# Attention after a convolution on one core: minus the maximum by one step of eight 32x64 tiles, dumps folded by DMAs, value halves added by TensorE

## What is computed

```
h = group_norm1(x, n2_g, n2_b)
q, k, v = conv1x1(h, q_w, q_b), conv1x1(h, k_w, k_b), conv1x1(h, v_w, v_b)   # each (B, 64, N)
attn = softmax(einsum('bnc,bcm->bnm', q, k) * 64 ** -0.5, axis=-1)           # (B, N, N)
out = x + einsum('bnm,bmc->bnc', attn, v)
```

## Time and profile before

| | |
|---|---|
| median of 3 runs | 3047.66 us (3044.29 to 3048.20) |
| the profiled execution | 3046.7 us |
| its span, first to last instruction | 3045.0 us |
| busy: TensorE / VectorE / ScalarE / GpSimd | 90% / 65% / 73% / 76% |
| granted TensorE clock, mean | 0.96 of full speed |

### The profile page before, as it was taken

The page is one execution under the profiler, slowest core; times in us unless marked ns, Lnnn a source line. Parts: engine busy times, 40 slices in busy tenths (PEclk is TensorE's granted clock), DMA queues, the critical chain, the costliest instruction groups (busy, mean ns, idle before and its releaser), DMA issues.

```text
span 3045.0 us, 87180 instructions
## 1 busy us (share of the span) xinstructions
PE 2736.0 (90%) x36568; PEld 1138.5 (37%) x36568; DVE 1967.6 (65%) x2081; ACT 2218.4 (73%) x2288; POOL 2311.9 (76%) x2056
## 2 busy tenths in 40 slices
PE   7898999998989898999988989999999999999998
PEld 4343333333333333333333333333333333333333
DVE  4766666666666666666657666666666666666665
ACT  4577777777777777777767777777777777777777
POOL 1467777777778787877865878787888888887886
PEclk9999999999999999999999999999999999999999
DMA  6148666666666666666601656666666666666561
GB/s 195 35 102 182 130 131 128 129 126 129 132 127 131 128 131 127 131 133 126 122 7 41 130 125 135 132 129 130 130 135 134 134 135 134 134 135 128 124 128 21
DMA packets 124020, 371.20 MB, mean 122 GB/s; under 512 B 17640, under 2 KB 43752, under 8 KB 123120
## 3 DMA queue, kind: packets, MB, share of 16 engines
q0 software_dynamic: 88128, 320.90, 51.8%
q1 hardware_dynamic: 35504, 44.75, 5.5%
HBM read 16.41 MB, written 9.44 MB: 8 GB/s over the span
## 4 chain that ended last, share of the span: by engine, by line
PE 36%; POOL 21%; issue 13%; DVE 11%; DMA 11%; ACT 6%; POOLq 0%; ACTq 0%; SPq 0%; DVEq 0%
POOL arena L486 17%; PE ps L1060 16%; PE ps L1049 12%; DMA accD<-arena 11%; DVE mxp L827 6%; PE ps L1069 5%; ACT arena L576 3%; POOL accD L501 2%; DVE arena L853 2%; POOL mseed L519 2%; ACT ps L617 2%; PE ps L1182 2%; DVE accD L850 1%; ACT pvx L591 1%; DVE pvc L874 1%
## 5 line engine op out<-in xcount | busy, mean ns | idle before, releaser
L827 DVE TENSOR_REDUCE mxp<-ps 128x1 f32<-128x1024 f32 x1296 | 1581.0, 1224 | 775.2 <-PE ps L1069 774.1
L486 POOL TENSOR_TENSOR arena<-arena 128x512 f32<-128x512 f32 x1224 | 1703.2, 1391 | 417.7 <-ACT arena L576 351.9
L576 ACT ACTIVATE arena<-ps,bnd 128x1024 f32<-128x1024 f32 x1296 | 1382.0, 1110 | 502.3 <-PE ps L1049 483.8
L1060 PE MATMUL ps<-arena,vals 64*64 64x512 f32 x10368 | 1294.6, 613 | 0.2 <-DVE pvc L874 0.2
L1049 PE MATMUL ps<-arena 64*64 64x512 f16 x15552 | 1087.0, 382 | 145.1 <-ACT ps L617 140.1
L617 ACT ACTIVATE ps<-mseed 128x1024 f32<-128x1024 f32 x612 | 628.8, 1027 | 176.6 <-POOL mseed L519 125.5
L1049 PEld LDWEIGHTS ps<-arena 64*64 64x64 f16 x15552 | 463.1, 108 | 589.8 <-issue 322.1
L1069 PE MATMUL ps<-arena,QM 64*64 64x512 f16 x5184 | 528.5, 395 | 121.8 <-DVE mxp L827 116.9
L501 POOL DMA_DIRECT2D accD<-arena x544 | 494.4, 910 | 94.2 <-DMA accD<-arena 56.4
L1060 PEld LDWEIGHTS ps<-arena,vals 64*64 64x64 f32 x10368 | 385.0, 137 | 419.9 <-issue 333.7
L1069 PEld LDWEIGHTS ps<-arena,QM 64*64 64x64 f16 x5184 | 153.5, 105 | 664.1 <-DVE mxp L827 574.3
(11 more groups left out here) (124 smaller groups left out, 807.1 us busy)
## 6 DMA issues: line engine op xcount, KB each, us to landing
accD<-arena POOLq DMA_DIRECT2D x612, 512.0 KB, 5.1
arena<-arena SPq DMA_DIRECT2D x144, 64.0 KB, 3.5
arena<-in_x_rows SPq DMA_DIRECT2D x8, 816.0 KB, 9.7
xs<-in_x SPq DMA_DIRECT2D x4, 1152.0 KB, 15.5
f_scratch<-arena SPq DMA_DIRECT2D x32, 144.0 KB
f<-f_scratch SPq DMA_DIRECT2D x16, 288.0 KB, 9.7
QM<-arena SPq DMA_DIRECT2D x72, 64.0 KB, 3.5
xst<-arena SPq DMA_DIRECT2D x72, 64.0 KB, 4.4
```

The lines of the kernel that those rows point to most:

```text
L486: nc.gpsimd.tensor_tensor(accA[:, n % 2, :], accA[:, n % 2, :], e, ALU.add).then_inc(adda_free, 1)
L576: nc.scalar.activation(E[:, :, slot_of(n % 2, p), :], ps[:, S_BANK + 2 * buf:S_BANK + 2 * buf + 2, :], ACT.Exp, scale=bnd[:, 6:7]).then_in ...
L827: nc.vector.reduce_max(flat(mxp[:])[:, v:v + 1], flat(ps[:, bank:bank + 2, :]), AX.X).then_inc(mx_free, 1)
L1060: a = nc.tensor.matmul(ps[C * t:C * t + C, ACC_BANK + r, :], V[rows, p, t, :], E[rows, t, slot_of(par, p), :], start=(p == 0), stop=(p == ...
```

## The change

`place_minus_maxima` takes the place of the fourth term and of all fills. One step of eight matmuls on tiles of 32 x 64 writes minus the maximum to the four score banks of both pairs of a turn, and three terms of each pair are added to it. It waits for the exponential of pair p+1 before it writes. `seed`, `fill_source`, `is_seeded` and `mseed` go.

Dumps are issued after each odd pair of their own block, into one of two `accD` by turns. In the next block, after pairs 5, 8 and 11 (`FOLD_AFTER`), GpSimd's queue issues three accumulating DMAs: half of `accD` onto the other, then its two parts onto `accA` (`fold_dumps`). `sum_dumps` goes, and `total` stays for the last block of a batch.

The row sums are taken at pair 18 instead of 12. Behind them TensorE adds the two halves of the values with weights `twice` (two identity matrices, one above the other) into the other half of the same bank (`value_sums`), and ScalarE copies both at once. `turn_pv` and `sum_pv` go. `add_pv` stands behind the first reduction of a block, not ahead of it. GpSimd multiplies after pair 31. VectorE's reciprocals come one a pair. In the stretch between the batches the same steps shift by some chunks (not shown), and at the very end VectorE multiplies straight from PSUM.

```diff
@@ -52,19 +52,19 @@
 K_ROWS = KW + 1
 
 AHEAD = 4
-ROW_SUMS = 12
+ROW_SUMS = 18
 
 LASTS = NBLK - 1
-DUMP_AFTER = (8, 9, 11, 12, 14, 15, 17, 18, 20, 21, 23, 25, 27, 29, 31, 33, 35, 35)
-NDUMP = len(DUMP_AFTER)
-DUMPS_SUMMED = 6
+NDUMP = NPAIR // 2
+FOLD_AFTER = (5, 8, 11)
+NFOLD = len(FOLD_AFTER)
 RECS = 8
-SEEDED = (0, 1)
 QK_TOP = 2.0 ** 14
 
 ROUNDING = 1.0 + 2.0 ** -10
 ONE = 2.0 ** 14
-M_ROW = 1.0 / (ONE * 64)
+ROWS = 32
+M_ROW = 1.0 / (ONE * ROWS)
 
 
 def program(nc, x, x_rows, conv_w, per_row, per_channel, matrices, matrices_t, out):
...
             def dump(b, j, g):
 
-                n, k = blk(b, j), g % 2
+                n, k, d = blk(b, j), g % 2, dumped_block(b, j)
                 at = slot_of(n % 2, 2 * g)
                 pool.wait_ge(e_ready, NPAIR * n + 2 * g + 3)
                 if g >= 2:
                     pool.wait_ge(dumped[k], dumps_before(b, j, g))
-                    pool.dma_start(accD[:, k, :], E[:, 1, at:at + 2, :].rearrange("p s c -> p (s c)"), accum_op=ALU.add
+                    pool.dma_start(accD[:, d % 2, k, :], E[:, 1, at:at + 2, :].rearrange("p s c -> p (s c)"), accum_op=ALU.add
                                    ).then_inc(dumped[k], 16)
                 else:
-                    if n:
-                        pool.wait_ge(accb_out, n)
-                    pool.dma_start(accD[:, k, :], E[:, 1, at:at + 2, :].rearrange("p s c -> p (s c)")).then_inc(dumped[k], 16)
-
-            def total(n):
-
+                    if d:
+                        pool.wait_ge(dumped[k], dumps_before(b, j, g))
+                    if d >= 2:
+                        pool.wait_ge(folded, folds_before(d - 1, 0))
+                    pool.dma_start(accD[:, d % 2, k, :], E[:, 1, at:at + 2, :].rearrange("p s c -> p (s c)")
+                                   ).then_inc(dumped[k], 16)
+
+            def fold_dumps(b, j, i):
+
+                n, d = blk(b, j), dumped_block(b, j)
+                if i == 0:
+                    for k in (0, 1):
+                        pool.wait_ge(dumped[k], dumps_before(b, j + 1, 0))
+                    pool.dma_start(accD[:, d % 2, 0, :], accD[:, d % 2, 1, :], accum_op=ALU.add).then_inc(folded, 16)
+                else:
+                    pool.wait_ge(folded, folds_before(d, i))
+                    pool.wait_ge(adda_free, NSLOT + NPAIR * (n + 1))
+                    pool.dma_start(accA[:, n % 2, :], accD[:, d % 2, 0, (i - 1) * CH:i * CH], accum_op=ALU.add
+                                   ).then_inc(folded, 16)
+
...
             def attend(b, j):
                 n = blk(b, j)
-                fill_source(n)
                 first_a(n)
-                for p in range(2, NPAIR):
-                    add_a(n, p)
-                    if j < LASTS:
-                        for g in range(NDUMP):
-                            if DUMP_AFTER[g] == p:
-                                dump(b, j, g)
-                    if j and p == DUMPS_SUMMED + 2:
-                        total(n - 1)
-                    if j and p == 33:
-                        pool.wait_ge(rec_ready, RECS * n)
-                        pool.wait_ge(pv_summed, 2 * n)
-                        nc.gpsimd.tensor_tensor(pvt[:], pvt[:], rec[:], ALU.mult).then_inc(norm_done, 1)
+                for p in range(1, NPAIR):
+                    if p > 1:
+                        add_a(n, p)
+                    if j < LASTS and p % 2:
+                        dump(b, j, p // 2)
+                    if j and p in FOLD_AFTER:
+                        fold_dumps(b, j - 1, FOLD_AFTER.index(p))
+                    if j and p == 31:
+                        normalize(n - 1)
...
                 nc.scalar.activation(flat(pvc[:]), ps[:, ACC_BANK, :], ACT.Copy).then_inc(acc_copied, 1)
-
-            def turn_pv(n):
-
-                act.wait_ge(acc_free, n + 1)
-                for h in (0, 1):
-                    nc.scalar.activation(pvx[C * h:C * h + C, :], pvc[C - C * h:2 * C - C * h, h, :], ACT.Copy).then_inc(pv_turned, 1)
 
             def copy_row_sums(n, bank):
                 act.wait_ge(rs_ready, n + 1)
                 if n:
                     act.wait_ge(rec_ready, RECS * n)
-                nc.scalar.activation(rsum[:], ps[:, bank, 0:HCH], ACT.Copy).then_inc(rs_copied, 1)
+                    act.wait_ge(norm_done, n)
...
                         copy_row_sums(n - 1, S_BANK)
-                    if p + 2 < NPAIR and is_seeded(b, p + 2):
-                        seed(b, j, p + 2)
                     if p == 1 and j:
                         move_pv(n - 1)
-                    if p == 4 and j:
-                        turn_pv(n - 1)
                     if p == NPAIR - 3 and j + 1 < NBLK:
                         widen_maxima(n + 1)
                     if p == NPAIR - 1 and j + 1 < NBLK:
...
                         add_b(b, n, p + 1)
-                    if j and p == 10:
-                        sum_pv(n - 1)
-                    if j and p == DUMPS_SUMMED:
...
@@ -1032,22 +1005,28 @@
                 pe.wait_ge(st_in, n + 2)
                 nc.tensor.matmul(ps[:, bank, 2:3], of[:], dev[:, 1:2], start=True, stop=True).then_inc(st_ps, 1)
 
-            def scores(par, p, peers, seeds=None):
+            def place_minus_maxima(par, peers):
 
                 if peers is not None:
                     pe.wait_ge(e_ready, peers + 1)
+                for r in (0, 2, 1, 3):
+                    rows = slice(ROWS * r, ROWS * r + ROWS)
+                    for h in (0, 1):
+                        cols = slice(C * h, C * h + C)
+                        nc.tensor.matmul(ps[cols, S_BANK + 2 * (r % 2) + r // 2, :], one16[rows, cols], QS[rows, par, 2, :],
+                                         start=True, stop=False, skip_group_check=True, tile_position=(ROWS * r, C * h))
+
+            def scores(par, p):
+
                 keys = slice(p * P, (p + 1) * P)
-                terms = ((KH[:, keys], 0), (KL[:, keys], 0), (KH[:, keys], 1), (one16[:], 2))
-                if seeds is not None:
-                    pe.wait_ge(seeded, seeds)
-                    terms = terms[:3]
+                terms = ((KH[:, keys], 0), (KL[:, keys], 0), (KH[:, keys], 1))
                 for k, (of, part) in enumerate(terms):
                     for t in (0, 1):
                         rows = slice(C * t, C * t + C)
                         for h in (0, 1):
                             cols = slice(C * h, C * h + C)
                             a = nc.tensor.matmul(ps[cols, S_BANK + 2 * (p % 2) + t, :], of[rows, cols], QS[rows, par, part, :],
-                                                 start=(k == 0 and seeds is None), stop=(k == len(terms) - 1),
+                                                 start=False, stop=(k == len(terms) - 1),
                                                  skip_group_check=True)
                 a.then_inc(s_ready, 1)
 
...
+
+            def value_sums(n, bank):
+                pe.wait_ge(acc_free, n + 1)
+                for h in (0, 1):
+                    a = nc.tensor.matmul(ps[C * h:C * h + C, bank, HCH:CH], twice[:], pvc[:, h, :], start=True, stop=True)
                 a.then_inc(rs_ready, 1)
 
-            def row_sums(n, bank):
-                pe.wait_ge(sum_ready, n + 1)
+            def row_sums(b, j, bank):
+                n = blk(b, j)
+                if j < LASTS:
+                    pe.wait_ge(folded, folds_before(dumped_block(b, j) + 1, 0))
+                    sums = accA[:, n % 2, :]
+                else:
+                    pe.wait_ge(sum_ready, b + 1)
+                    sums = accS[:]
                 for h in (0, 1):
-                    a = nc.tensor.matmul(ps[C * h:C * h + C, bank, 0:HCH], ones[:, 0:C],
-                                         accS[:, h * HCH:(h + 1) * HCH], start=True, stop=True)
-                a.then_inc(rs_ready, 1)
+                    nc.tensor.matmul(ps[C * h:C * h + C, bank, 0:HCH], ones[:, 0:C],
+                                     sums[:, h * HCH:(h + 1) * HCH], start=True, stop=True)
+                value_sums(n, bank)
 
             def attend(b, i, par, first=False, looks=2):
                 j = 2 * i + par
...
-                        scores(par, p + 2, n0 + p + 1)
-                        scores(par, p + 3, n0 + p + 2, seeds_before(b, j, p + 4) if is_seeded(b, p + 3) else None)
+                        place_minus_maxima(par, n0 + p + 2)
+                        scores(par, p + 2)
+                        scores(par, p + 3)
                     elif looks:
                         pe.wait_ge(m_ready, n + 2)
                         pe.wait_ge(qs_in[1 - par], staged)
-                        scores(1 - par, 0, n0 + p + 1)
-                        scores(1 - par, 1, n0 + p + 2)
+                        place_minus_maxima(1 - par, n0 + p + 2)
+                        scores(1 - par, 0)
+                        scores(1 - par, 1)
...
-                        row_sums(n - 1, S_BANK)
```

(8 more changed lines are left out.)

125 lines of the change are left out of this document (51 added, 74 removed).

## The result

| | before | after |
|---|---|---|
| median of 4 runs each, us | 3047.93 (3044.29 to 3051.62) | 2864.17 (2861.83 to 2866.19) |
| ratio | | 0.9397, 95% interval 0.9381 to 0.9413 |
| the profiled execution, us | 3046.7 | 2864.74 |
| its span, us | 3045.0 | 2863.0 |
| granted TensorE clock, mean | 0.96 | 0.994 |

The change takes 184 us off where 112 were forecast. 2864 lies within the range of 2850 to 3040, near its lower end.

The account below looks back on a forecast made before the run. TensorE was taken as the bound, with waits for fills at crossings. Middle blocks fall from 78.3 to 74.7 us: 3046.7 - 115 (32 blocks) + 11 (first blocks) - 8 (last blocks) = 2935 us, range 2850 to 3040.

Parts of the forecast that it names:

- What bounds the kernel: TensorE bounds quiet turns (3.67 us); blocks of 78.10 us hold 12.0 excess, mostly a crossing wait for fills from GpSimd's source.
- 10.2 us a block gone: Excesses of 7.04 (but for 0.3), 0.94, 2.01 and 0.47 vanish with fills, crossing copy and VectorE's adds.
- the 0.94 in ScalarE's turn: Excess of the two turns after the crossing, 959.47 to 967.75, counted as gone; no cause was given.
- the 0.47: Excess of two turns, 973.43 to 981.24, put down to VectorE adding the value halves and counted as gone.
- The backlog at the block's end has no source: GpSimd: dumps now begin at pair 1 in a second buffer, 66.6 us a block, under TensorE's, so no late backlog.
- The placing step, 0.35 a turn: Changing tile shape out and back costs 0.30, eight tiles 0.05; 6.3 us a block; bounds 0 and 0.56.
- The leftovers: Small excesses expected to stay in a block: crossing 0.3, row sums' turn 1.2, spread maxima about 0.8 us.
- Nothing for the wait for both exponentials: The placing step waits for both exponentials of the turn before; 0.46 us of cover remains, so costed at nothing.
- 7.04: Excess in us of the crossing into a block, with 3.33 idle for a fill and then a lower clock.
- the rival of new waits: Cover at the placing step used up or a fold late: 36 to 108 us more, 2971 to 3043; chance 0.18.
- Two rounds for eight tiles: Rival: the placing step's eight tiles run as two rounds, 0.21 more a step, 3071 us, slower; chance 0.12.
- No price for the tiles: Rival: changing tile shape at the placing step is free, 227 us less, about 2708; chance 0.10 including a half-free change.

Follow-up runs that it names:

- e8: The kernel before with one edit: ScalarE fills straight from the row of minus maxima (`QS`), GpSimd makes no source; 2857.13 us, ratio 0.9388.
- e4: The kernel before with a fourth term of four 64x64 matmuls for every pair, no fills and no source by GpSimd; 2894.75 us, ratio 0.9507.
- e5: The changed kernel with the fills of before, their source made by GpSimd in one buffer instead of two; 2789.89 us, ratio 0.9164.
- e3: The changed kernel with the placing step as four 32x64 tiles for the even pair alone, scores scaled by 0.01; 2856.83 us in one run.
- e2: The changed kernel with the placing step as four 64x64 tiles for the even pair alone, scores scaled by 0.01; 2723.67 us in one run.
- e1: The changed kernel with a fourth term of four 64x64 matmuls for each pair instead of the placing step, no fills; 2854.77 us, ratio 0.9376.
- e6: The changed kernel with ScalarE's fills for odd pairs from 3 on, straight from `QS`, without a source by GpSimd; 2751.53 us, ratio 0.9036.

## Why the prediction was right, and where its sizes were off

The direction and the mechanism held: the wait for the fills goes, the clock with it, and the placing step gives part of it back. Point by point:

- **What bounds the kernel.** Right. e8 removes the source of the fills alone and takes 6.0 us off a block. In the kernel before the views of waits and the clock agree on it: 3.7 us of waiting, and then slower matmuls.
- **"10.2 us a block gone".** Right in sum: 78.4 to 72.4 is 6.0 net, and 4.5 (18 x 0.25) plus 0.41 (the row sums' turn, 1.17 against 0.76) were given back; 0.28 came from the turns with the spread maxima. That makes 6.0 + 4.5 + 0.41 - 0.28 = 10.6. The split was less sure than I wrote: e4 shows that the 0.94 in ScalarE's turn came from the fills, and that most of the 0.47 goes while VectorE's adds stay.
- **"The backlog at the block's end has no source".** Half right. With the early dumps GpSimd still comes to the source 3.6 us after the maxima (e5), against 5.9 before. The change didn't need it, since its fills are gone.
- **The placing step, 0.35 a turn: the term that was mis-sized.** It costs 0.25. I had taken 0.30 from the earlier trace rows, which change between 64 and 128 rows, and 0.05 for the start of eight tiles from the earlier trace rows. Between 64 and 32 rows the price is 0.23 (e3) and four more tiles cost 0.013. The values behind the row sums took 0.05 longer in the earlier trace rows, and I counted that as a price of the shape; behind the placing step nothing takes longer. Over 648 turns 0.10 makes 65 of the 70 us between 2935 and the profiled 2865. The leftovers (15 us) and the crossings (10 the other way), both below, are the rest.
- **"Nothing for the wait for both exponentials".** Right (e2).
- **The leftovers.** Crossing 0.17 against 0.3, row sums 1.17 against 1.2, spread 0.50 against 0.8: 0.46 a block less, 15 us over 32 blocks. The crossing's is luck in part: GpSimd's first add starts 0.26 us behind VectorE's `ot` in the change and 0.04 behind it in e1, and there the crossing's excess is 0.9. Nothing in the prediction foresaw that.
- **The crossings are not all alike.** I priced all at 7.04. The median of the trace before is 7.2, but the crossing out of each batch's first block has an excess of 2.1. Some 5 us less to gain, twice. The turns of that block are longer (4.34 and 4.56 where it has more searches), so GpSimd may have more time in it; I didn't test that.
- **Block 1 of the first batch.** Not foreseen: 81.7 against 83.3 before, so it gains 1.6 where its neighbours gain 6.1. It is the rival of new waits, in one block of 34: a fold landed late, behind the loads for the second image. Only part of that is new, since this block was 5 us longer than its neighbours in the kernel before too, and is 9 longer now.
- **Two rounds for eight tiles.** Refuted: from its start to that of the scores the step takes 0.35, less than two rounds of 0.21 without any gap, and e3 prices four of the eight at 0.013. **No price for the tiles** is refuted by the gaps of 0.11 and 0.14.

What of the change is good, then? From e8 and e6, which share the direct fills: earlier dumps, folds and value sums take a block from 72.4 to 69.2. From e6 and after, which share those: the placing step in place of the fills takes it back from 69.2 to 72.4: 18 x 0.25 = 4.4 more, less 0.95 at the crossing (`ot` again) and 0.29 around the spread maxima. The title's part of the change, set against fills that work, loses 3.2 us a block; it seemed to gain because the fills before had a late source.

## What to carry to other kernels

When an engine waits for a small operand, ask first who makes it and whether the reader could take it straight from where it lies: one edit of ScalarE's source gained as much here as new arithmetic on TensorE, new queues and folds together. A step that packs more tiles into another shape than its neighbours' need not be cheaper; count the two changes of shape against the steps saved (here 0.24 with the tiles, against 0.20). And measure a term alone before building on its price: the nearest row of a trace may have the same mechanism and another size.

## What the runs showed of the hardware that I had not expected

**A change of tile shape costs a quarter of a microsecond out and back.** Between steps of 64x64 tiles, one step of 32x64 costs 0.23 us (e3), more than the plain step of 0.21 itself. For 128x64 it was 0.28 to 0.30 in the earlier trace rows, with 0.05 of that on the values behind and with other types and sizes; whether the price depends on the pair of shapes isn't shown.

**An add on GpSimd seems to hold an add on VectorE.** VectorE's `ot` takes 0.47 us alone and 1.59 where an add of GpSimd's starts 0.04 later (e1, e6). In every long case of e1 and e6 it ends 0.28 to 0.30 after an add of GpSimd's. Where GpSimd's add starts 0.26 later, in the change, it stays at 0.47, and an issue of a DMA beside it (e6, at 1010.57) doesn't lengthen it. The order alone isn't a rule yet: in two crossings of e6 GpSimd's add starts 0.23 and 0.32 later and `ot` is long all the same. What the runs do show is that a shift of 0.2 us between two engines that don't bound the kernel, from e1 to the change, is worth some 0.7 us of each block.

**A stall costs more than its length, through the clock.** The view of stretches of the kernel before, around the crossing of the earlier trace rows: stretch, its us, TensorE busy (instructions), granted clock, share of DMA, GB/s.

```profile
945.00:949.00 4.00, 4.00 (x67) 1.00 0.98 208
949.00:953.30 4.30, 1.02 (x20) 0.92 0.87 164
953.40:957.00 3.60, 2.81 (x24) 0.50 0.87 174
957.00:961.00 4.00, 4.00 (x48) 0.69 0.00 0
```

The timeline of TensorE in the last two of them:

```profile
955.64 0.64 PE L1069 MATMUL ps<-arena,QM 64*64 64x512 f16 x4 [0.79 <-DVE mxp L827]
956.06 3.57 PE L1060 MATMUL ps<-arena,vals 64*64 64x512 f32 x16
```

TensorE was busy 1.02 of 4.30 us. Then the granted clock is 0.50, the lower of its two levels (1.2 of 2.4 GHz), for a stretch in which it works again, and it is back only within the next. The values take 959.47 - 956.06 = 3.41 instead of 1.71, the 12 scores 1.28 instead of 0.64 (an estimate, twice the plain pace, as their row's 1.49 against 0.82 suggests), the search 0.2 more. So 3.33 us of waiting for the fill and 0.79 for VectorE cost 2.5 more through the clock. The shorter waits of e8 at its crossing (1.19 and 0.77) leave the matmuls behind them at their pace: 12 in 0.84.
